# Output projection of a gated cross-attention layer: partial sums kept in DRAM by accumulating transfers

## The chip, the core and the metric

The kernel runs on one core of one Trainium2 chip. The metric is the device time of one execution in microseconds. TensorE (PE) multiplies, VectorE (DVE), ScalarE (ACT) and GpSimd (POOL) work on tiles, SyncE (SP) issues transfers; they run beside each other and wait for one another by semaphores.

## What is computed

A layer with cross-attention and a low-rank expert layer, in fp32, over 16 batches of 128 tokens of width 1024. The change touches the last product of the first line and its sum with x:

```python
NUM_HEADS, NUM_KV_HEADS, HEAD_DIM, HIDDEN = 32, 8, 128, 1024
...
q = (hidden_states @ q_proj_w.T).reshape(B, Q, NUM_HEADS, HEAD_DIM).transpose(0, 2, 1, 3)
...
scores = jnp.einsum('bhqd,bhkd->bhqk', q, k) * scale + attention_mask
attn = jax.nn.softmax(scores.astype(jnp.float32), axis=-1).astype(q.dtype)
out = jnp.einsum('bhqk,bhkd->bhqd', attn, v)
out = out.transpose(0, 2, 1, 3).reshape(B, Q, NUM_HEADS * HEAD_DIM)
return out @ o_proj_w.T
...
x = x + jnp.tanh(g_xattn[0]) * _L0_xattn_ref(_layernorm(x, axis=-1), ctx_4096, ...)
x = x + jnp.tanh(g_ffn[0]) * _L0_ffn_ref(_layernorm(x, axis=-1), L0_ffn_A, L0_ffn_B, L0_ffn_Wr)
```

The gate tanh(g_xattn) is already in the heads when they are written, so the projection's results are added to x as they are.

## The kernel before

All large products are cut into 96 **entries** of one shape: activations of a pair of batches (two row blocks of 128) against a 1024 x 1024 block of weights. Each is done as seven products k = 0 to 6 of half size instead of eight, with sums of the operands taken before (`staged` combinations, by `sums` on GpSimd) and of the results after (`ev`, `usum`). Every operand is split into a high and a low part (`s_hi`, `s_lo` of the activations, `t_hi`, `t_lo` of the weights), and a product is 4 x 3 matmuls of 128 x 512 (lines 715 to 717). The results go to four PSUM banks, `BANK_OF = (0, 1, 2, 3, 0, 2, 3)`.

The entries stand in a fixed order: 16 for keys and values, 32 for queries (with the attention interleaved), 32 for the output projection (O0 to A0, q = 0 to 31), 8 and 8 for the experts. The output projection runs over four **slices** of the 4096 head columns, each over the 8 pairs: slice q // 8, with weights `t` that stay for 8 entries. The result of a pair is the sum over its four slices and x.

Each engine runs its own written-out order, entry by entry and within an entry by position j = 0 to 6, the number of the product that PE is at:

- PE does product k when `s_lo` and (in the first entry of a set) `t_lo` of k are there and the bank is free.
- SP refills the weights `t_raw[k]` (1 MB) in the last entry of a set, each when its product is done, since `t_raw` lies on `t_lo`; at j = 1 it issues the staging of the next entry (1 MB in two transfers, `staged`), all on one queue, and around it the stores and loads of sums.
- ACT casts `s_hi` and `t_hi`, and takes product 0 into `ev`.
- VectorE subtracts for `s_lo` and `t_lo`, and takes the products 1 to 6 out of the banks.
- GpSimd makes the sums of the staged activations, and adds `usum` twice and `ev` once to the sums of the pair.

The seven weights of a new set are due at positions 4, 5, 6 of the set's last entry and 0, 2, 3, 4 of the next (`FILL_POSITIONS`).

The running sums of a pair (1 MB) are in one of two SBUF buffers `acc`, loaded before the entry (`sums_in`, in two halves, from x in slice 0) and stored after it (`sums_out`). The order of the pairs turns round at each slice (`pair_of`), so that the last two pairs of a slice are the first two of the next and stay in SBUF: at q % 8 = 6 and 7 nothing is stored, at 0 and 1 nothing is loaded. q = 0 and 1 write their results without adding; their x is added in DRAM later by `x_into_sums`, two accumulating transfers per pair from GpSimd's queue. After the last slice the rows are normalised and transposed (`finish`).

## Time and profile before

| | us |
|---|---|
| median of 3 executions | 2381.99 (2379.24 to 2382.4) |
| profiled execution | 2379.71 |
| its span, first to last instruction | 2377.9 |
| output projection, q = 2 to 31 | 1391 to 2012 of the span |
| PE busy | 2278.4 (96%) |
| VectorE, ScalarE, GpSimd busy | 1611.9, 1172.6, 1317.3 |

The profile is of one execution. Busy time of an engine is the time in which one of its instructions runs; the matmuls of PE are pipelined and overlap, so their distance from start to start counts, not their length. Where an engine sat idle before an instruction, the view names what ended the wait. "issue" is a wait for which the profile shows no releaser.

### The profile page before, as it was taken

The page shows a single profiled execution, that of the slowest core. Times are in us where ns is not written, and L with a number is a line of the kernel's source. Part 1 is how long each engine was busy: PE and PEld are TensorE (multiplying, and loading weights), DVE is VectorE, ACT ScalarE, POOL GpSimd, SP SyncE. Part 2 cuts the span into 40 slices and gives each one's busy share as a digit, 9 for nine tenths or more (in the row PEclk, how much of TensorE's full clock was granted, in tenths as well). Part 3 has the DMA queues.
Part 4 walks back from the last instruction along what each step waited for, and adds up shares of the span by engine and source line. Part 5 has one row for each costly group of instructions (what it writes and reads, how often), then busy time and mean ns, then how long its engine had stood idle before and what let it go on. Part 6 is the DMA issues. An engine that isn't in the chain of part 4 may idle for free.

```text
span 2377.9 us, 35655 instructions
## 1 busy us (share of the span) xinstructions
PE 2278.4 (96%) x11600; PEld 1911.7 (80%) x11600; DVE 1611.9 (68%) x2649; ACT 1172.6 (49%) x3751; POOL 1317.3 (55%) x1823
## 2 busy tenths in 40 slices
PE   5998999999999989999999899899899999999899
PEld 4886887888888878888888788688687787788687
DVE  6557557777777797777777845755756877544755
ACT  4546546666666676666666722422423334332421
POOL 5566668655565566555555645554655765434321
PEclk8999999999999999999999999999999999999999
DMA  4687556757757457642222545555456466324643
GB/s 170 217 228 268 187 159 231 216 163 198 197 165 198 131 193 195 194 126 89 89 93 95 191 165 177 203 180 202 151 168 238 142 210 253 121 72 144 228 169 133
DMA packets 180231, 412.98 MB, mean 174 GB/s; under 512 B 12176, under 2 KB 77968, under 8 KB 164624
## 3 DMA queue, kind: packets, MB, share of 16 engines
q1 hardware_dynamic: 175440, 379.24, 46.6%
q0 software_dynamic: 4608, 31.46, 7.4%
q8 instruction: 95, 1.56, 0.3%
q14 instruction: 88, 0.72, 0.1%
HBM read 293.21 MB, written 178.26 MB: 198 GB/s over the span
## 4 chain that ended last, share of the span: by engine, by line
PE 86%; POOL 4%; issue 3%; DVE 3%; DMA 3%; ACT 1%; SPq 0%; POOLq 0%; ACTq 0%; DVEq 0%
PE bank L715 24%; PE bank L717 23%; PE bank L716 23%; PE bank L773 4%; PE bank L781 2%; PE bank L761 2%; PE bank L798 1%; PE bank L797 1%; PE bank L796 1%; DVE t_lo L1239 1%; DMA staged<-heads 1%; POOL staged L1696 1%; POOL s_hi L1706 1%; DMA staged<-in_w_q 1%; PE bank L813 1%
## 5 line engine op out<-in xcount | busy, mean ns | idle before, releaser
L715 PE MATMUL bank<-t_hi,s_hi 128*128 128x512 f32 x2688 | 1091.3, 406 | 81.1 <-issue 42.7
L717 PE MATMUL bank<-t_hi,s_lo 128*128 128x512 f32 x2688 | 1059.3, 394 | 0.0
L716 PE MATMUL bank<-t_lo,s_hi 128*128 128x512 f32 x2688 | 1056.1, 393 | 0.0
L715 PEld LDWEIGHTS bank<-t_hi,s_hi 128*128 128x128 f32 x2688 | 510.3, 190 | 189.0 <-issue 85.4
L1239 DVE TENSOR_TENSOR s_lo<-staged,s_hi 128x512 fp32r<-128x512 f32 x672 | 538.2, 846 | 99.6 <-ACT s_hi L962 92.0
L717 PEld LDWEIGHTS bank<-t_hi,s_lo 128*128 128x128 f32 x2688 | 508.8, 189 | 112.0
L716 PEld LDWEIGHTS bank<-t_lo,s_hi 128*128 128x128 f32 x2688 | 510.9, 190 | 91.0
L962 ACT CAST s_hi<-staged 128x512 fp32r<-128x512 f32 x434 | 250.2, 623 | 342.7 <-DMA staged<-heads 181.0
L1679 POOL TENSOR_SCALAR small<-small 128x4 f32<-128x4 f32 (+1 forms) x192 | 66.3, 345 | 414.5 <-ACT small L1051 338.4
L1694 POOL TENSOR_TENSOR staged<-staged 128x512 f32<-128x512 f32 x96 | 139.3, 1451 | 271.1 <-DMA staged<-heads 97.6
L1239 DVE TENSOR_TENSOR t_lo<-t_raw,t_hi 128x2048 fp32r<-128x2048 f32 x70 | 183.2, 2625 | 34.2 <-ACT t_hi L951 25.1
L1364 DVE SCALAR_TENSOR_TENSOR probs<-bank,small,mask 128x128 f32<-128x128 f32 x512 | 144.1, 343 | 89.6 <-POOL small L1686 43.8
L1057 ACT ACTIVATE probs<-probs,small 128x128 f32<-128x128 f32 x512 | 197.5, 386 | 14.1 <-DVE small L1368 14.1
L1045 ACT ACTIVATE bank<-bank 128x128 f32<-128x128 f32 x512 | 135.6, 265 | 113.8 <-PE bank L761 113.8
L1768 POOL TENSOR_TENSOR sums<-sums,usum 128x512 f32<-128x512 f32 x60 | 91.4, 1544 | 175.6 <-DVE usum L1253 175.6
L1038 ACT ACTIVATE heads<-bank,small 128x512 f32<-128x512 f32 x128 | 88.2, 689 | 185.1 <-PE bank L798 183.9
L971 ACT COPY ev<-bank 128x512 f32<-128x512 f32 x96 | 56.1, 585 | 203.5 <-PE bank L717 191.6
L1706 POOL CAST s_hi<-staged 128x512 fp32r<-128x512 f32 x238 | 153.8, 716 | 1.3 <-PE bank L717 1.3
L1696 POOL TENSOR_TENSOR staged<-staged 128x512 f32<-128x512 f32 x96 | 146.9, 1531 | 7.5
L1697 POOL TENSOR_TENSOR staged<-staged 128x512 f32<-128x512 f32 x96 | 150.1, 1563 | 0.0
L773 PEld LDWEIGHTS bank<-keys,queries 128*128 128x128 f32 x1024 | 133.5, 191 | 14.0 <-issue 4.8
L1700 POOL TENSOR_TENSOR staged<-staged 128x512 f32<-128x512 f32 x96 | 137.9, 1436 | 0.0
(131 smaller groups left out, 2961.7 us busy)
## 6 DMA issues: line engine op xcount, KB each, us to landing
heads<-heads SPq DMA_DIRECT2D x128, 256.0 KB, 3.7
t_raw<-combos SPq DMA_DIRECT2D x28, 1024.0 KB, 10.2
t_raw<-in_sets SPq DMA_DIRECT2D x25, 1024.0 KB, 9.6
staged<-in_w_q SPq DMA_DIRECT2D x32, 768.0 KB, 5.9
staged<-heads SPq DMA_DIRECT2D x32, 768.0 KB, 5.9
sums<-sums SPq DMA_DIRECT2D x18, 1024.0 KB, 7.9
sums<-sums SPq DMA_DIRECT2D x36, 512.0 KB, 4.6
xt<-x_columns SPq DMA_DIRECT2D x8, 1792.0 KB, 7.2
```

What stands on the lines that cost most here:

```text
L715: nc.tensor.matmul(out, s_hi[w][:, cols], high, start=start, stop=False, skip_group_check=True)
L716: nc.tensor.matmul(out, s_hi[w][:, cols], low, start=False, stop=False, skip_group_check=True)
L717: done = nc.tensor.matmul(out, s_lo[w][:, cols], high, start=False, stop=at == 3, skip_group_check=True)
L773: done = nc.tensor.matmul(bank[6][:, b * S:b * S + S], qt[j][:, b, :], kg[blk][:, b, :], start=True, stop=True)
L962: nc.scalar.copy(s_hi[k][:, :], staged[:, k, :]).then_inc(s_hi_done, 1)
L1057: done = nc.scalar.activation(pr[i % 3][:, b, :], pr[i % 3][:, b, :], ACT.Exp, bias=nmax[w][:, b:b + 1], accum_out=rsum[w][:, b:b + 1])
L1239: return nc.vector.tensor_tensor(out, whole, hi.bitcast(FP32), ALU.subtract)
L1364: done = nc.vector.scalar_tensor_tensor(pr[i % 3][:, b, :], bank[6][:, b * S:b * S + S], q_rstd[w][:, b:b + 1], mask[:, :], ALU.mult, ALU.add)
L1694: nc.gpsimd.tensor_tensor(staged[:, 2, :], staged[:, 3, :], staged[:, 6, :], ALU.subtract).then_inc(s_sum, 1)
L1696: nc.gpsimd.tensor_tensor(staged[:, 1, :], staged[:, 2, :], staged[:, 0, :], ALU.subtract).then_inc(s_sum, 1)
L1697: nc.gpsimd.tensor_tensor(staged[:, 3, :], staged[:, 0, :], staged[:, 3, :], ALU.subtract).then_inc(s_sum, 1)
L1706: nc.gpsimd.tensor_copy(s_hi[k][:, :], staged[:, k, :]).then_inc(s_hi_done, 1)
```

## The change

In the slices 0 to 2 (`in_dram(q)`, q < 24) an entry no longer adds to sums in SBUF. It writes its own results into `acc[q % 2]` as q = 0 and 1 did (products 3, 5, 6 by VectorE, product 4 now by a copy on ACT), and GpSimd's queue adds the tile to the pair's sums in DRAM by one accumulating transfer of 1 MB. The sums in DRAM are first set to x, by 16 transfers of 0.5 MB that SP issues during the query entries n = 18 to 25. GpSimd's three additions per entry, the stores, the loads of the slices 0 to 2 and `x_into_sums` are gone. In the last slice the sums are loaded for all eight pairs, in one transfer each, and the additions stay. All slices take the pairs in the same order. Semaphores, buffer parities and the tiles laid over `acc` later follow from this.

```diff
     def pair_of(q):
-        return 7 - q % 8 if (q // 8) % 2 else q % 8
-    def sums_loaded(q):
-        return q % 8 >= 2
+        return 7 - q % 8
+    def in_dram(q):
+        return q < 24
     def parts_added(q):
-        return 3 * max(q - 1, 0)
-    def sums_stored(q):
-        return q < 24 and q % 8 < 6
-    def sums_before(q):
-        return q - (1 if q % 8 == 0 else 3)
+        return 3 * (q - 23)
+    def added_before(q):
+        return min(q, 24 + q % 2) // 2
     def loads_up_to(q):
-        return len([p for p in range(q + 1) if sums_loaded(p) and pair_of(p) % 2 == pair_of(q) % 2])
-    def stores_before(q):
-        return len([p for p in range(q) if sums_stored(p) and pair_of(p) % 2 == pair_of(q) % 2])
+        return (q - 24) // 2 + 1
...
-        def sums_out(q):
-            e, b = O0 + q, pair_of(q) % 2
-            for c, k in ((0, 4), (2, 5), (3, 6)):
-                sp.wait_ge(taken[c], plan.after[e, k])
-            if parts_added(q):
-                sp.wait_ge(o_sum, parts_added(q))
-            sp.dma_start(d.sums[pair_of(q)], acc[b][:, :, :]).then_inc(acc_out[b], 16)
+        def sums_start(i):
+            for w in range(2):
+                out = d.sums[i, :, 2 * w:2 * w + 2, :].rearrange("p c q -> p (c q)")
+                sp.dma_start(out, d.x[tiles(i)[w]]).then_inc(sums_set, 16)
         def sums_in(q):
-            b = pair_of(q) % 2
+            b = q % 2
             if q < 26:
-                sp.wait_ge(acc_out[b], 16 * stores_before(q))
+                sp.wait_ge(acc_out[b], 16 * added_before(q))
             else:
                 sp.wait_ge(f_norm, 2 * (q - 25))
-                sp.wait_ge(f_out[q % 2], 32 * ((q - 26) // 2 + 1))
-            if q in (14, 15):
-                sp.wait_ge(x_added[pair_of(q)], 32)
-            for w in range(2):
-                half = acc[b][:, 2 * w:2 * w + 2, :]
-                if q < 8:
-                    sp.dma_start(half.rearrange("p c q -> p (c q)"), d.x[tiles(pair_of(q))[w]]).then_inc(acc_in[b], 16)
-                else:
-                    sp.dma_start(half, d.sums[pair_of(q), :, 2 * w:2 * w + 2, :]).then_inc(acc_in[b], 16)
+                sp.wait_ge(f_out[b], 32 * ((q - 26) // 2 + 1))
+            sp.dma_start(acc[b][:, :, :], d.sums[pair_of(q)]).then_inc(acc_in[b], 16)
...
                     combo_copy(e, r == 3)
-                if n == 33 and r == 2:
-                    sums_out(0)
-                if n == 33 and r == 3:
-                    sums_in(2)
+                if 18 <= n < 26 and r == 0:
+                    sums_start(n - 18)
         heads_out(127)
...
                     stage(e + 1, e)
-                    if sums_stored(q - 1):
-                        sums_out(q - 1)
-                if j == (3 if q < 25 else 5) and q < 31 and sums_loaded(q + 1):
+                if j == (3 if q < 24 else 5) and 23 <= q < 31:
                     sums_in(q + 1)
...
                 act.wait_ge(taken[3], plan.after[e - 1, 3])
-                if O0 + 2 <= e - 1 < A0:
+                if O0 + 24 <= e - 1 < A0:
                     act.wait_ge(o_sum, parts_added(e - 1 - O0))
...
             act.wait_ge(prod, plan.prod[O0 + q, 4])
-            act.wait_ge(s_done, 128 if q else 126)
-            nc.scalar.copy(acc[q][:, 0, :], bank[0][:, :]).then_inc(taken[0], 1)
+            if q < 2:
+                act.wait_ge(s_done, 128 if q else 126)
+            else:
+                act.wait_ge(acc_out[q % 2], 16 * added_before(q))
+            nc.scalar.copy(acc[q % 2][:, 0, :], bank[0][:, :]).then_inc(taken[0], 1)
...
                     first_product(e)
+                if j == 4 and in_dram(q):
+                    sums_tile(q)
                 fill_s(e, after_start(e, j))
...
         def sums_tile(q, k):
-            if k != 5 or q == 0:
+            if q >= 2:
+                dve.wait_ge(acc_out[q % 2], 16 * added_before(q))
+            elif k != 5 or q == 0:
                 if k == 6 and q:
                     dve.wait_ge(pt_done, 127)
                 else:
                     dve.wait_ge(s_done, {3: 128 if q else 125, 5: 126, 6: 127}[k])
             at = {3: 3, 5: 1, 6: 2}[k]
-            {3: result22, 5: result12, 6: result21}[k](O0 + q, acc[q][:, at, :])
+            {3: result22, 5: result12, 6: result21}[k](O0 + q, acc[q % 2][:, at, :])
...
-            b, e = pair_of(q) % 2, O0 + q
+            b, e = q % 2, O0 + q
             at = {3: 3, 4: 0, 5: 1, 6: 2}[k]
             dve.wait_ge(prod, plan.prod[e, k])
-            if k == 3 and sums_loaded(q):
-                dve.wait_ge(acc_in[b], 32 * loads_up_to(q))
-            elif k == 3:
-                dve.wait_ge(o_sum, parts_added(sums_before(q)))
-            if k == 4 and not sums_loaded(q):
-                dve.wait_ge(taken[0], plan.after[O0 + sums_before(q), 4])
+            if k == 3:
+                dve.wait_ge(acc_in[b], 16 * loads_up_to(q))
             if k > 4:
                 dve.wait_ge(o_sum, parts_added(q - 1) + k - 4)
             (minus if k == 3 else plus)(acc[b][:, at, :], acc[b][:, at, :], k)
         def rows2(f, w):
-            b, e, n = (7 - f) % 2, O0 + 24 + f, 2 * f + w
+            b, e, n = f % 2, O0 + 24 + f, 2 * f + w
             if w:
...
             for j in SEVEN:
-                if j == 0 and q == 2:
-                    sums_tile(1, 6)
-                if j == 0 and q > 2:
-                    add_sums(q - 1, 6)
+                if j == 0:
+                    (sums_tile if in_dram(q - 1) else add_sums)(q - 1, 6)
                 if j == 1:
                     second_product(e)
                 if j == 2:
                     third_product(e)
-                if j in (3, 4, 5):
+                if j in (3, 5) and in_dram(q):
+                    sums_tile(q, j)
+                if j in (3, 4, 5) and not in_dram(q):
                     add_sums(q, j)
...
-            b, e = pair_of(q) % 2, O0 + q
+            b, e = q % 2, O0 + q
             if j == 1:
-                if sums_loaded(q):
-                    pool.wait_ge(acc_in[b], 32 * loads_up_to(q))
-                else:
-                    pool.wait_ge(taken[2], plan.after[O0 + sums_before(q), 5])
-                    pool.wait_ge(taken[3], plan.after[O0 + sums_before(q), 6])
+                pool.wait_ge(acc_in[b], 16 * loads_up_to(q))
                 pool.wait_ge(taken[1], plan.after[e, 1])
...
-        def x_into_sums(i):
-            pool.wait_ge(acc_out[i], 16)
-            for w in range(2):
-                nc.gpsimd.dma_start(d.sums[i, :, 2 * w:2 * w + 2, :].rearrange("p c q -> p (c q)"), d.x[tiles(i)[w]],
-                                    accum_op=ALU.add, max_dma_last_dim=4096).then_inc(x_added[i], 16)
+        def sums_out(q):
+            b, e = q % 2, O0 + q
+            for c, k in ((0, 4), (2, 5), (3, 6)):
+                pool.wait_ge(taken[c], plan.after[e, k])
+            if q == 0:
+                pool.wait_ge(sums_set, 256)
+            if q >= 2:
+                pool.wait_ge(acc_out[b], 16 * added_before(q))
+            nc.gpsimd.dma_start(d.sums[pair_of(q)], acc[b][:, :, :], accum_op=ALU.add, max_dma_last_dim=8192).then_inc(acc_out[b], 16)
...
                 finish(plan.beat0[e] + j)
-                if j == 1:
+                if j == 1 and in_dram(e - O0 - 1):
+                    sums_out(e - O0 - 1)
+                if j == 1 and not in_dram(e - O0):
                     add_sums(e - O0, j)
-                if j == 5 and e - O0 in (5, 6):
-                    x_into_sums(e - O0 - 5)
                 if j == 3:
                     sums(e + 1)
-                    add_sums(e - O0, j)
+                    if not in_dram(e - O0):
+                        add_sums(e - O0, j)
                     if e == O0 + 10:
```

Where the instructions stand now is seen at the change from slice 1 to slice 2 (q = 15 to 16). ACT, before: from its cast of weights 3 on, through the first entry of the new slice.

```order
L951 CAST t3_hi_58<-t3_raw_60 128x2048 [waits t_in3]
L962 CAST s_hi_70<-staged_72 128x512 [waits staged_in,product]
L951 CAST t4_hi_61<-t4_raw_63 128x2048 [waits t_in4]
L951 CAST t5_hi_64<-t5_raw_66 128x2048 [waits t_in5]
L951 CAST t6_hi_67<-t6_raw_69 128x2048 [waits t_in6]
L962 CAST s_hi_70<-staged_72 128x512 [waits staged_in,product]
```

ACT, in the changed kernel, the same place.

```order
L931 CAST t3_hi_58<-t3_raw_60 128x2048 [waits t_in3]
L942 CAST s_hi_70<-staged_72 128x512 [waits staged_in,product]
L931 CAST t4_hi_61<-t4_raw_63 128x2048 [waits t_in4]
L931 CAST t5_hi_64<-t5_raw_66 128x2048 [waits t_in5]
L1009 COPY sums0_112<-bank0 128x512 [waits sums_out0,product]
L931 CAST t6_hi_67<-t6_raw_69 128x2048 [waits t_in6]
```

The copy of product 4 (bank 0) of q = 16 now stands between the casts of weights 5 and 6; likewise the copy of q = 15 stands before the cast of weights 0. VectorE, before: from the low part of weights 4 to the result of product 5 of q = 16.

```order
L1239 TENSOR_TENSOR t4_lo_62<-t4_raw_63,t4_hi_61 128x2048 [waits t_hi_done]
L1257 TENSOR_TENSOR sums0_112<-sums0_112,bank3 128x512 [waits o_sum,product]
L1239 TENSOR_TENSOR t5_lo_65<-t5_raw_66,t5_hi_64 128x2048 [waits t_hi_done]
L1253 TENSOR_TENSOR sums0_112<-sums0_112,bank0 128x512 [waits taken_a,product]
L1239 TENSOR_TENSOR t6_lo_68<-t6_raw_69,t6_hi_67 128x2048 [waits t_hi_done]
L1253 TENSOR_TENSOR sums0_112<-sums0_112,bank2 128x512 [waits o_sum,product]
```

VectorE, in the changed kernel.

```order
L1224 TENSOR_TENSOR t4_lo_62<-t4_raw_63,t4_hi_61 128x2048 [waits t_hi_done]
L1242 TENSOR_TENSOR sums0_112<-ev_73,bank3 128x512 [waits taken_c,product,sums_out0]
L1224 TENSOR_TENSOR t5_lo_65<-t5_raw_66,t5_hi_64 128x2048 [waits t_hi_done]
L1224 TENSOR_TENSOR t6_lo_68<-t6_raw_69,t6_hi_67 128x2048 [waits t_hi_done]
L1246 TENSOR_TENSOR sums0_112<-bank2,usum_74 128x512 [waits product,sums_out0]
```

The result of product 4 is gone from between the low parts of weights 5 and 6. GpSimd, before: one entry, from the sums of the staged activations on.

```order
L1694 TENSOR_TENSOR staged_72<-staged_72 128x512 [waits staged_in]
L1696 TENSOR_TENSOR staged_72<-staged_72 128x512 [waits s_sum]
L1697 TENSOR_TENSOR staged_72<-staged_72 128x512
L1700 TENSOR_TENSOR staged_72<-staged_72 128x512 [waits s_sum,staged12_in]
L1771 TENSOR_TENSOR sums0_112<-sums0_112,ev_73 128x512 [waits taken_d]
L1768 TENSOR_TENSOR sums1_113<-sums1_113,usum_74 128x512 [waits taken_b,taken_d,taken_c]
```

GpSimd, in the changed kernel.

```order
L1677 TENSOR_TENSOR staged_72<-staged_72 128x512 [waits staged_in]
L1679 TENSOR_TENSOR staged_72<-staged_72 128x512 [waits s_sum]
L1680 TENSOR_TENSOR staged_72<-staged_72 128x512
L1683 TENSOR_TENSOR staged_72<-staged_72 128x512 [waits s_sum,staged12_in]
L1761 DMA sums<-sums0_112 128x2048 [waits taken_d,sums_out0,taken_c,taken_a]
```

The additions are gone; the issue of the accumulating transfer waits for the last result tile of the entry before and stands ahead of the sums of the next.

## Rows read from the trace of the kernel before

**Rows 1.** The page: busy us (share of span) and instructions of each engine.

```profile
PE 2278.4 (96%) x11600; PEld 1911.7 (80%) x11600; DVE 1611.9 (68%) x2649; ACT 1172.6 (49%) x3751; POOL 1317.3 (55%) x1823
```

**Rows 2.** Windows: stretch, length, busy of PE, PEld, DVE, ACT, POOL, clock, DMA.

```profile
1391.00:1551.00 160.00, 153.31 (x658) 124.85 (x657) 95.29 (x107) 45.59 (x66) 85.64 (x59) 0.98 0.57 186
1551.00:1716.00 165.00, 157.53 (x689) 128.51 (x688) 105.12 (x115) 51.60 (x75) 91.92 (x60) 1.00 0.52 179
...
870.00:1150.00 280.00, 278.97 (x1635) 241.94 (x1634) 212.32 (x431) 183.66 (x780) 165.23 (x310) 1.00 0.51 141
```

**Rows 3.** Timeline of SP's queue: start, length, refills behind products 0 and 1.

```profile
1488.83 0.33 SPq L437 DMA_DIRECT2D t_raw<-in_sets  x1
...
1652.37 0.33 SPq L437 DMA_DIRECT2D t_raw<-in_sets  x1
...
1655.09 0.32 SPq L437 DMA_DIRECT2D t_raw<-combos  x1
...
1813.82 0.33 SPq L437 DMA_DIRECT2D t_raw<-in_sets  x1
```

**Rows 4.** Timeline of PE: first matmuls of products; in brackets idle before.

```profile
1512.72 0.77 PE L715 MATMUL bank<-t_hi,s_hi 128*128 128x512 f32 x1 [3.26 <-issue]
...
1532.32 0.47 PE L715 MATMUL bank<-t_hi,s_hi 128*128 128x512 f32 x1 [0.29 <-issue]
...
1674.19 0.47 PE L715 MATMUL bank<-t_hi,s_hi 128*128 128x512 f32 x1 [2.81 <-issue]
...
1687.21 0.47 PE L715 MATMUL bank<-t_hi,s_hi 128*128 128x512 f32 x1 [1.51 <-issue]
...
1693.80 0.47 PE L715 MATMUL bank<-t_hi,s_hi 128*128 128x512 f32 x1 [0.30 <-issue]
...
1835.17 0.47 PE L715 MATMUL bank<-t_hi,s_hi 128*128 128x512 f32 x1 [2.03 <-issue]
...
1854.77 0.47 PE L715 MATMUL bank<-t_hi,s_hi 128*128 128x512 f32 x1 [0.30 <-issue]
```

**Rows 5.** Timeline of ACT: casts that waited for the staging, casts of weights.

```profile
1504.58 0.62 ACT L962 CAST s_hi<-staged 128x512 fp32r<-128x512 f32 x1 [6.32 <-DMA staged<-heads]
...
1665.08 0.62 ACT L962 CAST s_hi<-staged 128x512 fp32r<-128x512 f32 x1 [6.03 <-DMA staged<-heads]
...
1679.19 5.52 ACT L951 CAST t_hi<-t_raw 128x2048 fp32r<-128x2048 f32 x3
...
1824.93 0.62 ACT L962 CAST s_hi<-staged 128x512 fp32r<-128x512 f32 x1 [4.25 <-DMA staged<-heads]
```

**Rows 6.** Timeline of VectorE at T2.

```profile
1674.02 2.38 DVE L1239 TENSOR_TENSOR s_lo<-staged,s_hi 128x512 fp32r<-128x512 f32 x2
1676.32 2.28 DVE L1239 TENSOR_TENSOR t_lo<-t_raw,t_hi 128x2048 fp32r<-128x2048 f32 x1
...
1679.12 1.28 DVE L1239 TENSOR_TENSOR s_lo<-staged,s_hi 128x512 fp32r<-128x512 f32 x2
...
1684.32 2.78 DVE L1239 TENSOR_TENSOR t_lo<-t_raw,t_hi 128x2048 fp32r<-128x2048 f32 x1
...
1690.32 0.67 DVE L1253 TENSOR_TENSOR sums<-sums,bank 128x512 f32<-128x512 f32 x1
```

**Rows 7.** Timeline of GpSimd at T2: its additions to the sums.

```profile
1671.91 3.33 POOL L1771 TENSOR_TENSOR sums<-sums,ev 128x512 f32<-128x512 f32 x1
1683.37 4.88 POOL L1768 TENSOR_TENSOR sums<-sums,usum 128x512 f32<-128x512 f32 x2 [8.13 <-DVE usum L1253]
```

**Rows 8.** The page, DMA queues: packets, MB, share of 16 engines; q0 is GpSimd's.

```profile
q1 hardware_dynamic: 175440, 379.24, 46.6%
q0 software_dynamic: 4608, 31.46, 7.4%
```

**Rows 9.** GpSimd's issues from x at T1; the landings of all transfers on combos.

```profile
1488.37 1.64 POOL L1777 DMA_DIRECT2D sums<-in_x  x2
```

```profile
DMA to landing us min/median/max: 4.8/9.0/15.0
```

More of the change, by code:

```diff
@@ L296, in program @@
     end = max(end, m.at)
-    ring = [m.over(f"ranks{w}", [P, HALF], acc_at + (w + 4) % 8 * HALF * 4) for w in range(8)]
+    ring = [m.over(f"ranks{w}", [P, HALF], acc_at + w * HALF * 4) for w in range(8)]
     gc = m.over("gated_columns", [P, 4, HALF], xr2_at)
     yr = [[m.over("y_rows00", [P, HIDDEN], xo2_at), m.over("y_rows01", [P, HIDDEN], xo2_at + HIDDEN * 4)],
-          [m.over("y_rows10", [P, HIDDEN], acc_at + 2 * HIDDEN * 4), m.over("y_rows11", [P, HIDDEN], acc_at + 3 * HIDDEN * 4)]]
+          [m.over("y_rows10", [P, HIDDEN], acc_at), m.over("y_rows11", [P, HIDDEN], acc_at + HIDDEN * 4)]]
     ct = [m.over(name, [P, HALF], rw_at + w * HALF * 4) for w, name in enumerate(("c22", "c12", "c21"))]
@@ L328, in program @@
     acc_in, acc_out = [sem(f"sums_in{w}") for w in range(2)], [sem(f"sums_out{w}") for w in range(2)]
-    x_added = [sem(f"x_added{w}") for w in range(2)]
+    sums_set = sem("sums_set")
     o_sum, f_out = sem("o_sum"), [sem(f"f_out{w}") for w in range(2)]
@@ L556, in finish @@
                     for w in range(2):
-                        sp.dma_start(d.x2[tiles(p)[w]], acc[p % 2][:, 2 * w:2 * w + 2, :].rearrange("p c q -> p (c q)")).then_inc(f_out[f % 2], 16)
+                        sp.dma_start(d.x2[tiles(p)[w]], acc[f % 2][:, 2 * w:2 * w + 2, :].rearrange("p c q -> p (c q)")).then_inc(f_out[f % 2], 16)
                 if at == 9:
@@ L1413, in normalise2 @@
         def normalise2(f, w):
-            b = (7 - f) % 2
+            b = f % 2
             dve.wait_ge(f_step, 5 * (2 * f + w + 1))
@@ L1830, in _ @@
                     queries(i)
+                if n == 33 and r == 1:
+                    sums_out(0)
                 if r == 2:
```

## Prediction, made before the changed kernel was run

> **What bounds the kernel now.** I read the page first: TensorE (PE) is busy 96% of the span, the other engines 49 to 68% [rows 1]. A change that takes work from VectorE (DVE) and GpSimd (POOL) can therefore only win where PE waits for them. So the next view was the table of windows over the first two slices of the output projection [rows 2]: PE is idle 6.7 and 7.5 us (160 less 153.31, 165 less 157.53; matmuls overlap, so more is lost than this). Then PE's own instructions there, looking for gaps in their starts. A product of 12 matmuls takes 2.72 us (the refills behind products 0 and 1, 1652.37 and 1655.09, [rows 3]), an entry of seven 19.0, and the only gaps of PE are around q = 7, 15 and 23, where the next entry's products need new weights. I call these T1, T2 and T3.
>
> At each, everything is counted from R, the issue of the first refill of weights, which comes when product 0 of the slice's last entry is done: 1488.83, 1652.37 and 1813.82 [rows 3]. Twelve products of 2.72 later, at R + 32.7 with no idle, PE should start the last product (6) of the new slice's first entry. It starts it at 1532.32, 1693.80 and 1854.77 [rows 4], that is at R + 43.5, 41.4 and 41.0: 10.8, 8.7 and 8.3 us are lost, 28 us in all, and that is all that the three slices can give back.
>
> The loss has two parts. The first is **the landing L of the next entry's activations** (staged), seen where ScalarE (ACT) stops waiting for that DMA: 1504.58, 1665.08, 1824.93 [rows 5], or R + 15.75, 12.7 and 11.1. From L the sums on GpSimd, ACT's cast of k = 1, its cast of weights 1 and VectorE's low part follow one another, and product 1 starts at 1512.72, 1674.19 and 1835.17 [rows 4]: L + 8.1, 9.1 and 10.2. The second is **VectorE's chain from product 1 to product 6**: it is 19.6 us in all three (1532.32 - 1512.72, 1693.80 - 1674.19, 1854.77 - 1835.17), against 13.6 us of PE's five products. VectorE has no gap in it [rows 6].
>
> **What the change takes from the chain.** In the slices 0 to 2 GpSimd's three additions per entry go, and VectorE's result of product 4 becomes a copy on ACT. In ordinary entries this is worth nothing: PE has no idle there. In the chain of T2 I read [rows 6, 7]: the pair of low parts at 1674.02 takes 2.38 us beside GpSimd's addition of 1671.91 to 1675.24; such a pair takes 1.28 us when GpSimd is quiet (1679.12), so 1.1 us goes. The weights' low part at 1684.32 takes 2.78 beside the additions of 1683.37, and the next of its kind takes the same (two alike, one row stands); at 1676.32 with GpSimd quiet it is 2.28: twice 0.5. The result of product 4 at 1690.32 delays what is behind it by 0.6. Together 2.7 us, which would make 16.9 of 19.6.
>
> But the order on ACT gives most of it back. Before, its casts of weights 4, 5 and 6 stand in one row and are done early. Now the copy of product 4 of the new entry stands before the cast of weights 6, so that cast waits until PE has done product 4. From PE's start of product 4: product 2.7, copy 0.6, cast 1.9 [rows 5], low part 2.3, product 6 starts at + 7.5, where now it is 6.6 (1693.80 less 1687.21) [rows 4]. Product 4 itself comes at 13.0 after product 1 now (1687.21 - 1674.19) and at 13.0 - 1.1 - 0.5 = 11.4 then. **The chain is 11.4 + 7.5 = 18.9 at T1 and T2**, a gain of 0.7 and not 2.7. At T3 the new slice is the last, which keeps its additions and VectorE's result of product 4, so neither the copy nor the other gains are there, only the 1.1: 18.5. From L to product 1 I take 8.3: the new landing (below) is later, when VectorE's first low part of weights is done, as at T1 (8.1) and not as at T2 and T3 (9.1, 10.2). That low part itself moves, since ACT now casts weights 0 behind its copy of product 4 (R + 10.9): cast done at R + 13.4, low part at R + 15.7. Product 0 needs it and starts later, but product 1 waits longer anyway, so this costs nothing as long as L is above about R + 15; below it would cost up to 1 us.
>
> The slower of two passes on the shared memory port fits a rule: the Trainium skill, SBUF — State Buffer, section SBUF: two separate sides, says that VectorE with two SBUF inputs and a GpSimd instruction that reads SBUF exclude one another for the whole instruction. By this rule the gain is that of the missing GpSimd instructions alone, and the 2.28 against 2.78 us agrees in sign, though not with a full block.
>
> **What the change adds.** The store and the load of sums (2 MB an entry, plain) become one accumulating transfer of 1 MB. Its price: the accumulating queue moved 30 transfers of 1 MB (28 of combos, 2 from x) with 7.4% of 16 engines' span [rows 8], 0.074 x 2377.9 / 30 = 5.9 us each; the plain queue needed 0.466 x 2377.9 / 379.24 = 2.9 us per MB, 3.1 for the 1.05 MB of one transfer. So an accumulation holds the engines about as long as the store and the load did together, and in an ordinary entry (19 us, one staging of 3 us) all of it hides. Nothing waits for it soon: buffer q % 2 is written again 30 us later.
>
> But before, the order of the pairs left entries 7, 8, 15, 16, 23 and 24 without a store, and 8, 9, 16, 17, 24 and 25 without a load. Now **an accumulation starts in every one of the transition entries**, about 2 us ahead of the first refill: POOL issues it when VectorE has written the last tile of entry q - 1, R - 2.3, and needs 0.8 us for one [rows 9]. About 1.4 us of it run before the refills; the other 4.5 share the engines with refills 0 and 1 and delay the staging behind them on SP's queue. Added to T3's 11.1, the one with nothing in the way, this gives L = R + 15.6. T1 already shows the case: the two transfers from x are issued at 1488.37, half a us before R [rows 9], and L is R + 15.75; they go, and so does the load of sums in front of them, so with the earlier start of 0.9 us it gives 14.9. T2 would be 12.7 + 4.5 = 17.2 at most. I take 15.3 for all three. If the transfer from SBUF cost only the plain 3.1, 1.7 would be left: 12.8 from T3. So L lies between R + 12.8 and 17.2.
>
> For T3, the load of the sums of q = 24 comes too, behind refill 3; refill 6 lands later by 3 us, and VectorE reaches it at R + 39, so it is covered. The load of q = 25 (after the accumulation of q = 23, R + 35, landing at R + 42) is wanted at R + 50. The start of the sums, 16 transfers of 0.5 MB from x into DRAM, goes to 870 to 1150 us, where PE is busy 279.0 of 280 us and waits for no DMA [rows 2]; from 0 to 3 us, I take 0.5. GpSimd's new waits (for VectorE's last tile) stand in front of its sums for the next entry, whose data come 10 us later; nothing of those is held up.
>
> **The sum.** Start of product 6 after the change, from R: T1 and T2 15.3 + 8.3 + 18.9 = 42.5, T3 15.3 + 8.3 + 18.5 = 42.1. Against 43.5, 41.4 and 41.0: -1.0, +1.1, +1.1, together +1.2; with +0.5, **+1.7 us**. The profiled execution took 2379.71 (span 2377.9), the median of three is 2381.99; I add to the median: 2383.7. A measurement of this kernel can tell about 0.2%, 4.8 us, from no change.
>
> **Rivals.** (1) *Slower: the staging lands later than I think.* Each us of L counts three times. The sum is zero at L = R + 14.7 and slower by over 4.8 us from L = R + 16.3. At R + 17.2, T2's upper bound for all three, it is +7.4: 2389.4. For it: accumulations took up to 15.0 us from issue to landing [rows 9]. Against: T1 had the same megabyte starting later and landed at 15.75. A lowered clock may come with the longer idle of PE (the stretch of T1 has a mean granted clock of 0.98, the one of T2 1.00 [rows 2]), but the chain behind T1 was 19.6 us all the same, so it is hidden again.
> (2) *Faster: an accumulation out of SBUF costs no more than a plain transfer.* L = R + 12.8, the sum 1.7 - 7.5 = -5.8: 2376.2. Against it stand the 5.9 us; for it only that those all came from DRAM. The Trainium skill, DMA: Bandwidth & Descriptors, section Anatomy of one DMA, fits 2.0 us plus bytes at 436 GB/s for a transfer issued by GpSimd and has no surcharge for accumulating; by it a megabyte holds the engines 2.4 us, which is this rival, and the queue's row speaks against it.
> (3) *The chain does not shrink at all*, because an ACT cast or a refill sets its pace: 0.7 + 0.7 + 1.1 more, +4.2: 2386.2. Against: VectorE has no gap in it up to product 4, so what is taken from it there must come out.
>
> **Chances.** Forecast (L within 14 and 16.2, sum -2.2 to +4.4): 0.50. Rival 1 with L above 16.3: 0.24. Rival 2 and what lies toward it: 0.16, of which 0.13 pass -4.8. Rival 3: 0.10, half of it over +4.8 by the spread of L. From these: faster by over 0.2% 0.13, within 0.2% 0.58, slower 0.29. The range goes from 2375.5 to 2390, the lower end at rival 2, the upper at rival 1; the forecast's own is 2380 to 2386.5.
>
> **What would show it.** Right: a start of product 6 near R + 42 at all three, earlier than now at T1 and later at T2 and T3; L near R + 15; the pair of low parts at 1.3 us and a wait of VectorE for ACT before the last low part of weights; accumulations of 5 to 6 us of engine time each. Wrong: any gap of PE in an ordinary entry, a GpSimd or ACT wait for a sums transfer, PE losing time between 870 and 1150 us, or L outside 12.8 to 17.2.

## The result: slower by about 6 us

The changed kernel takes 2387.09 us, median of 13 executions (2383.62 to 2393.8), and the kernel before 2381.25 (13 executions, 2378.55 to 2384.92). The ratio is 1.003, 95% interval 1.0021 to 1.0038: slower by 5.0 to 9.0 us. The same kernel again, 8 executions on another occasion, gave 2389.0 against 2380.97, a ratio of 1.0035 (1.0024 to 1.0045). The forecast was 2383.7, likeliest within 0.2%. Both medians lie outside the forecast's own 2380 to 2386.5, and both are over 0.2% slower than before; they are inside the whole range of 2375.5 to 2390, whose upper end was set by a rival that did not occur.

### The profile page after: what moved, and what is told of

It is laid out like the page before. It is cut to its first block, busy times and chain, and to the rows that moved or that the text cites. A ratio compares the mean times of both kernels' runs of the same rounds, so it can differ in the third digit from the quotient of the medians.

```text
span 2392.0 us, 35572 instructions
## 1 busy us (share of the span) xinstructions
PE 2291.0 (96%) x11600; PEld 1922.1 (80%) x11600; DVE 1582.6 (66%) x2627; ACT 1182.1 (49%) x3773; POOL 1218.7 (51%) x1777
## 3 DMA queue, kind: packets, MB, share of 16 engines
q0 software_dynamic: 7488, 54.53, 12.6%
## 4 chain that ended last, share of the span: by engine, by line
PE 86%; DVE 3%; issue 3%; POOL 3%; DMA 3%; ACT 2%; SPq 0%; POOLq 0%; ACTq 0%; DVEq 0%
PE bank L695 24%; PE bank L697 24%; PE bank L696 24%; PE bank L753 4%; PE bank L761 2%; PE bank L741 2%; DVE t_lo L1224 1%; PE bank L778 1%; PE bank L777 1%; PE bank L776 1%; DVE s_lo L1224 1%; DMA staged<-heads 1%; DMA staged<-in_w_q 1%; ACT t_hi L931 1%; POOL staged L1679 1%
## 5 line engine op out<-in xcount | busy, mean ns | idle before, releaser
L1224 DVE TENSOR_TENSOR s_lo<-staged,s_hi 128x512 fp32r<-128x512 f32 x672 | 523.5, 824 | 115.6 <-ACT s_hi L942 107.1
L1677 POOL TENSOR_TENSOR staged<-staged 128x512 f32<-128x512 f32 x96 | 130.5, 1360 | 421.6 <-DMA staged<-heads 245.6
L1680 POOL TENSOR_TENSOR staged<-staged 128x512 f32<-128x512 f32 x96 | 149.6, 1558 | 0.0
L1679 POOL TENSOR_TENSOR staged<-staged 128x512 f32<-128x512 f32 x96 | 145.2, 1512 | 7.5
L1683 POOL TENSOR_TENSOR staged<-staged 128x512 f32<-128x512 f32 x96 | 142.7, 1486 | 0.0
L753 PE MATMUL bank<-keys,queries 128*128 128x128 f32 x1024 | 135.3, 275 | 1.6 <-DVE probs L1351 1.6
## 6 DMA issues: line engine op xcount, KB each, us to landing
t_raw<-combos SPq DMA_DIRECT2D x28, 1024.0 KB, 11.8
```

The costliest lines, as they stand in the source:

```text
L753: done = nc.tensor.matmul(bank[6][:, b * S:b * S + S], qt[j][:, b, :], kg[blk][:, b, :], start=True, stop=True)
L1224: return nc.vector.tensor_tensor(out, whole, hi.bitcast(FP32), ALU.subtract)
L1679: nc.gpsimd.tensor_tensor(staged[:, 1, :], staged[:, 2, :], staged[:, 0, :], ALU.subtract).then_inc(s_sum, 1)
L1680: nc.gpsimd.tensor_tensor(staged[:, 3, :], staged[:, 0, :], staged[:, 3, :], ALU.subtract).then_inc(s_sum, 1)
L1683: nc.gpsimd.tensor_tensor(staged[:, 5, :], staged[:, 4, :], staged[:, 1, :], ALU.add).then_inc(s_sum, 1)
```

## The profile after

The page of the changed kernel, engines and queues (as [rows 1, 8]), and its issues of accumulations (count, KB each, median us to landing):

```profile
PE 2291.0 (96%) x11600; PEld 1922.1 (80%) x11600; DVE 1582.6 (66%) x2627; ACT 1182.1 (49%) x3773; POOL 1218.7 (51%) x1777
...
q1 hardware_dynamic: 169392, 351.97, 42.9%
q0 software_dynamic: 7488, 54.53, 12.6%
...
sums<-sums POOLq DMA_DIRECT2D x24, 1024.0 KB, 8.0
```

The work went as meant: VectorE is busy 29 us less, GpSimd 99 us less, 27 MB fewer pass the plain queue. GpSimd's queue holds 52 transfers of 1 MB where it held 30: the 24 new ones, the 28 of combos, and no longer the two from x. They hold the engines 0.126 x 2392.0 / 52 = 5.8 us each on average; with the 28 at 5.9 as before, the 24 out of SBUF come to 5.7 each, as forecast. None of this is where the time is made; PE's busy time went up by 12.6 us with the same 11600 matmuls, so matmuls ran longer. The windows over the first two slices, columns as in [rows 2], show that and the clock:

```profile
1391.00:1551.00 160.00, 152.28 (x645) 124.14 (x645) 86.27 (x101) 48.89 (x72) 51.66 (x41) 0.96 0.55 150
1551.00:1716.00 165.00, 157.10 (x664) 127.97 (x663) 88.87 (x103) 53.48 (x80) 53.35 (x41) 0.96 0.53 147
```

The granted clock is 0.96 in both, where before it was 0.98 and 1.00. SP's queue dates the transitions T1, T2 and T3, and the next refill of weights after them, in the last entry of the last slice, called T4 here (as [rows 3]):

```profile
1490.88 0.34 SPq L431 DMA_DIRECT2D t_raw<-in_sets  x1
...
1657.69 0.33 SPq L431 DMA_DIRECT2D t_raw<-in_sets  x1
...
1825.02 0.33 SPq L431 DMA_DIRECT2D t_raw<-in_sets  x1
...
1997.10 0.33 SPq L431 DMA_DIRECT2D t_raw<-in_sets  x1
```

From R of T1 to that of T4 it is 506.2 us; before it was 495.9 (163.5 + 161.5 + 170.9). This is 10.3 of the 14.1 us between the two profiled executions (spans 2392.0 and 2377.9). Of the rest 2.1 us lie before T1 and 1.7 behind T4. This execution was the slowest of its 13. The second profiled execution of the same kernel has a span of 2386.6, 8.7 more than before: 4.1 from T1 to T4 (500.0 us), 4.2 before T1 and 0.4 behind T4. What lies before T1 is mostly scatter: the last matmul of the attention stage starts 1389.2 to 1393.4 us after the start in the eleven profiles of all kernels here, and the profile before is the earliest. Its mean is 1390.8 in the three profiles of the kernel before and its variants and 1392.0 in the eight of the changed kernel and its variants, so up to about 1.2 us may belong to the change; that is not shown. The differences of the medians, +5.8 and +8.0, lie between the +4.1 and the +10.3 of the two profiles from T1 to T4.

PE's products 1, 4 and 6 at T1 (compare [rows 4]), with the second and third matmul of product 6:

```profile
1514.51 0.77 PE L695 MATMUL bank<-t_hi,s_hi 128*128 128x512 f32 x1 [3.26 <-issue]
...
1526.02 0.47 PE L695 MATMUL bank<-t_hi,s_hi 128*128 128x512 f32 x1 [0.31 <-issue]
...
1534.91 0.76 PE L695 MATMUL bank<-t_hi,s_hi 128*128 128x512 f32 x1 [3.09 <-issue]
1535.47 0.63 PE L696 MATMUL bank<-t_lo,s_hi 128*128 128x512 f32 x1
1535.90 0.63 PE L697 MATMUL bank<-t_hi,s_lo 128*128 128x512 f32 x1
```

Product 6 comes after an idle of 3.09 us, which was 0.29 before, and from its second matmul on they start 0.43 us apart: 512 columns at 1.2 GHz. The chain to it, on ACT in the timeline:

```profile
1529.06 0.59 ACT L1009 COPY sums<-bank 128x512 f32<-128x512 f32 x1 [6.94 <-PE bank L697]
1529.54 1.91 ACT L931 CAST t_hi<-t_raw 128x2048 fp32r<-128x2048 f32 x1
```

On VectorE:

```profile
1531.48 3.33 DVE L1224 TENSOR_TENSOR t_lo<-t_raw,t_hi 128x2048 fp32r<-128x2048 f32 x1 [2.76 <-ACT t_hi L931]
```

And on GpSimd, which sums the next entry's activations:

```profile
1531.39 1.27 POOL L1679 TENSOR_TENSOR staged<-staged 128x512 f32<-128x512 f32 x1
1532.63 3.33 POOL L1680 TENSOR_TENSOR staged<-staged 128x512 f32<-128x512 f32 x1
```

ACT stood 6.94 us for product 4 with the cast of weights 6 behind it, as the forecast said; VectorE then waited 2.76 us for that cast. Its low part took 3.33 us and not 2.3. GpSimd was in an addition until 1532.66, and 1532.66 + 2.2 is when the low part is done; GpSimd's next addition, which takes 1.3 us when VectorE does not hold it up, took 3.33, that is until 1.2 us after the low part. In the second execution this addition of GpSimd starts at R + 39.4 and not R + 40.5, and ends 0.2 us after the low part has begun. GpSimd's timeline there:

```profile
1532.47 1.29 POOL L1679 TENSOR_TENSOR staged<-staged 128x512 f32<-128x512 f32 x1
```

VectorE's timeline in the second execution:

```profile
1533.57 2.35 DVE L1224 TENSOR_TENSOR t_lo<-t_raw,t_hi 128x2048 fp32r<-128x2048 f32 x1 [2.77 <-ACT t_hi L931]
```

And PE's, the first matmul of product 6:

```profile
1536.02 0.47 PE L695 MATMUL bank<-t_hi,s_hi 128*128 128x512 f32 x1 [2.12 <-issue]
```

Product 6 came at R + 42.97 there (R was 1493.05) after an idle of 2.12, at full clock. The rule of the Trainium skill that the prediction quoted (SBUF — State Buffer, section SBUF: two separate sides: VectorE with two SBUF inputs and a GpSimd instruction that reads SBUF exclude one another for a whole instruction) is borne out by these rows. The prediction read [rows 6] as less than a full block, and that was wrong: at T2 before, the low part began at 1684.32, the GpSimd addition that was running (1683.37, 1.59 us) ended at 1684.96, and 0.6 us of rest and 2.2 of its own make the 2.78. The same timeline of VectorE has a third such low part, that of weights 6:

```profile
1690.92 2.78 DVE L1239 TENSOR_TENSOR t_lo<-t_raw,t_hi 128x2048 fp32r<-128x2048 f32 x1
```

It began while GpSimd's first sum of the next entry's activations was running (1688.21, 3.34 us), 0.6 us before its end, and those sums stay in the changed kernel.

The windows of 10 us from product 6 on, at T1 and T2, show what the clock did. The kernel before:

```profile
1532.00:1542.00 10.00, 9.71 (x44) 8.03 (x44) 9.71 (x11) 3.92 (x7) 6.69 (x5) 1.00 0.00 0
1694.00:1704.00 10.00, 10.00 (x45) 8.26 (x45) 9.40 (x10) 3.91 (x7) 6.69 (x5) 1.00 0.01 2
```

The changed kernel:

```profile
1534.00:1544.00 10.00, 9.09 (x28) 7.32 (x29) 6.08 (x7) 1.19 (x3) 4.51 (x3) 0.66 0.13 13
1701.00:1711.00 10.00, 8.97 (x27) 7.13 (x28) 5.11 (x7) 0.34 (x1) 2.94 (x2) 0.66 0.13 15
```

Its second execution:

```profile
1536.00:1546.00 10.00, 9.98 (x44) 8.30 (x45) 7.69 (x10) 2.77 (x5) 3.63 (x3) 1.00 0.33 53
...
1699.00:1709.00 10.00, 9.72 (x36) 7.94 (x37) 6.73 (x9) 2.77 (x5) 3.88 (x3) 0.83 0.27 41
```

All together, us from R:

| | forecast | profile after T1; T2; T3 | second profile |
|---|---|---|---|
| staging landed | 15.3 | 15.1; 15.6; 15.1 | 15.3; 15.7; 15.5 |
| product 1 | 23.6 | 23.6; 23.8; 23.6 | 23.6; 23.9; 23.7 |
| product 6 | 42.5; 42.5; 42.1 | 44.0; 44.3; 42.1 | 43.0; 43.3; 42.2 |
| product 6 to next R, less before's | 0 | +2.7; +3.0; 0.0 | 0.0; +1.5; 0.0 |

Product 6 of the changed kernel comes +0.5, +2.9 and +1.2 us later than before, the lower clock behind it adds 2.7 and 3.0: 10.3, the whole difference. In the second execution -0.52, +1.82, +1.23 and +1.55 give 4.1. Two experiments below keep ACT's order and fit: there the stretch behind product 6 is 0.0 us longer at a granted clock of 1.00, 1.5 and 1.8 at 0.83, and 2.8 at 0.70.

## Experiments

**The same kernel again**, for a second profile:

> The changed kernel as it is, for a second profile: the first one came from its slowest execution (2393.8 where the median is 2387.1). If the 3 us at the lower clock behind T1 and T2 belong to the change, they are there again (stretches of 166 to 167.5 us from R to the next R, against 163.5 and 161.5 before), and the rest of the span is that of before, so about 2387. If they were an accident of that execution, the stretches are 164 and the total is nearer to 2384.

2389.0 us (2386.03 to 2392.78, 8 executions); its profile is read above. The time is that of the first case, but the stretches of the profiled execution are not: 163.0 from T1 to T2, with no lower clock, and 164.8 from T2 to T3. So the loss at the lower clock comes and goes from one execution to the next.

**1. The copy behind the cast.** The changed kernel, with ACT's copy of product 4 moved behind the cast of weights 6.

```diff
-                if j == 4 and in_dram(q):
-                    sums_tile(q)
                 fill_s(e, after_start(e, j))
...
                 fill_t(plan.beat0[e] + j)
+                if j == 4 and in_dram(q):
+                    sums_tile(q)
```

> The changed kernel with one edit: in an entry of the slices 0 to 2 ACT's copy of product 4 stands behind its cast of weights of the same position, not before it. Theory A (the cast of weights 6 that waits for product 4 is what costs): at T1 and T2 the time from product 1 to product 6 goes from 20.4 us to about 17, the idle of 3.1 us before product 6 goes, and with it the 3 us that PE loses behind it at the lower clock. Two times (3.4 + 2.9) = 12.6 us off: about 5 to 7 us faster than before, near 2375. Rival B (the time goes to the accumulations beside the refills, the order of ACT is hidden): L stays at R + 15 and the time at 2385 to 2388.

2379.54 us (2376.97 to 2381.92, 11), ratio to before 0.9996 (0.9987 to 1.0005), and 7.5 us less than the changed kernel. That is the kernel before again and not the 5 to 7 us faster that were expected. The staging lands where it did (R + 15.3, 16.1, 15.3). ACT's timeline at T1:

```profile
1528.89 0.59 ACT L1009 COPY sums<-bank 128x512 f32<-128x512 f32 x1 [5.01 <-PE bank L697]
```

VectorE's:

```profile
1526.29 4.48 DVE L1224 TENSOR_TENSOR t_lo<-t_raw,t_hi 128x2048 fp32r<-128x2048 f32 x2
```

The copy waits as before, but the last two low parts stand in one row (2.2 us each) without a wait, PE has no idle before product 6, and the stretches T1 to T2 and T2 to T3 take 160.5 and 161.3 us where after took 166.8 and 167.3. Less 120.0 from product 6 to the next R, product 6 of T1 is at R + 40.4, 16.9 after product 1 (R + 23.5), and that of T2 17.1 after it: the 16.9 that the prediction had for the chain without ACT's order. Most of what was gained at the chains is lost by the late landing, which stays as in the changed kernel: product 6 is 3.1 us earlier than before at T1, 0.1 at T2 and 1.1 later at T3, so from T1 to T4 it is 493.8 us against 495.9. So the order of two ACT instructions made the slowdown.

**2. The wait alone, in the kernel before.** ACT waits for product 4 before it casts weights 6, at q = 8 and 16:

```diff
                 fill_s(e + 1, before_next(e, j))
+                if j == 4 and q in (8, 16):
+                    act.wait_ge(prod, plan.prod[e, 4])
                 fill_t(plan.beat0[e] + j)
```

> The kernel before with one wait added: in the first entries of slices 1 and 2 (q = 8, 16) ACT waits for product 4 before it casts weights 6. No transfer and no addition changes. Theory A: product 6 starts 7.5 to 9 us after product 4 and not 6.6, with an idle of about 3 us before it, and PE loses 3 us at the lower clock behind it: +4 to +5 us at each, 2389 to 2391 where before is 2381. Rival B (the wait is hidden): no difference, 2381.

2383.12 us (2381.38 to 2387.78, 11), ratio 1.0008 (1.0 to 1.0017): +2 us (0 to 4), far less than the 8 to 10 expected. Product 6 at T1 in PE's timeline:

```profile
1536.40 0.47 PE L715 MATMUL bank<-t_hi,s_hi 128*128 128x512 f32 x1 [1.67 <-issue]
```

The two windows of 10 us behind product 6, at T1 and T2:

```profile
1536.00:1546.00 10.00, 9.60 (x42) 7.99 (x43) 9.01 (x11) 2.77 (x5) 5.11 (x4) 1.00 0.00 0
1699.00:1709.00 10.00, 9.81 (x43) 8.18 (x44) 8.96 (x11) 2.77 (x5) 5.13 (x4) 1.00 0.01 2
```

The wait moved product 6 by 1.0 and 1.4 us (R + 44.5 and 42.8), 2.4 us in all, which agrees with the measured 2, and the clock stayed at 1.00 after an idle of 1.67 us. Here the rest of the chain is slow too, so product 4 is late and the wait for it opens a short hole. In the changed kernel the low parts ahead are done sooner, the hole is 2.1 to 3.1 us, and what was saved comes out as idle. The expectation had wrongly given this wait the price of the clock as well.

**3. The start of the sums.** The kernel before with the 16 copies of x into (unused) DRAM that the change adds, issued by SP for the eight entries from 18 on:

```diff
+                if 18 <= n < 26 and r == 0:
+                    spare_start(n - 18)
```

> The kernel before with the 16 transfers of 0.5 MB from x into DRAM added in the query entries n = 18 to 25, into a buffer that nobody reads. Prediction's price: 0 to 3 us, 0.5 taken. Theory A (hidden): within 0.5 us of before, PE's busy time from 870 to 1150 us stays at 279. Rival B (the profiled 2 us that the changed kernel is late at 1371 us come from these): +2 us, and the last matmul of the attention starts at 1371.7, not 1369.8.

2380.68 us (2378.29 to 2386.13, 11), ratio 1.0005 (0.9996 to 1.0014). They cost nothing that can be told (the interval goes from -1 to +3.3 us). From 870 to 1150 us PE waits 2.5 us in all where before it waited 1.0, each time for VectorE and not for a transfer.

**4. A plain store instead of an accumulation.** The changed kernel without the adding, so the sums lack x and the other slices:

```diff
-            nc.gpsimd.dma_start(d.sums[pair_of(q)], acc[b][:, :, :], accum_op=ALU.add, max_dma_last_dim=8192).then_inc(acc_out[b], 16)
+            nc.gpsimd.dma_start(d.sums[pair_of(q)], acc[b][:, :, :]).then_inc(acc_out[b], 16)
```

> The changed kernel with plain stores in place of the accumulating ones, on the same queue and at the same places: the sums in DRAM hold only the last slice stored, so this leaves out the additions of x and of two slices. Theory A (an accumulation holds the DMA engines twice as long as a plain transfer of its size): L goes from R + 15.1 to about 12.5 to 13.5, product 1 comes 2 us earlier at T1 to T3, and the time falls by about 6 us to 2381. The wait of the cast of weights 6 for product 4 stays, and so the idle of 3 us before product 6 at T1 and T2. Rival B (it is the order on the queues, not the price of adding): L stays at 15 and the time at 2387.

2385.99 us (2382.9 to 2387.97, 7), ratio 1.0024 (1.0013 to 1.0035): the interval overlaps the changed kernel's, though a gain of 6 us was expected. GpSimd's queue on the page:

```profile
q0 software_dynamic: 7488, 54.53, 9.6%
```

GpSimd's first sum at T1, where R is 1492.48:

```profile
1504.33 1.30 POOL L1677 TENSOR_TENSOR staged<-staged 128x512 f32<-128x512 f32 x1 [12.32 <-DMA staged<-heads]
```

ACT's cast of weights 0:

```profile
1503.85 1.91 ACT L931 CAST t_hi<-t_raw 128x2048 fp32r<-128x2048 f32 x1
```

VectorE's low part of them:

```profile
1505.80 3.35 DVE L1224 TENSOR_TENSOR t_lo<-t_raw,t_hi 128x2048 fp32r<-128x2048 f32 x1 [4.40 <-ACT t_hi L931]
```

And product 6 on PE:

```profile
1534.96 0.52 PE L695 MATMUL bank<-t_hi,s_hi 128*128 128x512 f32 x1 [2.94 <-issue]
```

A plain megabyte costs 3.0 us less ((0.126 x 2392.0 - 0.096 x 2386.2) / 24), 2.7 for 5.7, and the staging lands 3.2 us sooner, at R + 11.9 (13.0 at T2). The price was right, its worth was not: with the landing there, ACT is casting weights 0, and VectorE's low part of them meets GpSimd's sums (3.35 us against 2.3). Product 6 comes at R + 42.5 and 43.3, 1.5 and 1.0 us before the profile after, and 0.5 before and level with its second one, and the idle before it, 2.94 us, is still ACT's order. So the accumulation's longer transfer is not what made the change slow.

**5. Accumulations behind the transition.** At q = 7, 15 and 23 GpSimd issues the accumulation behind its sums of the next entry's activations, and SP loads the sums of q = 24 at j = 6 instead of 3; with experiment 1's order on ACT, and without it.

```diff
-                if j == 1 and in_dram(e - O0 - 1):
+                if j == 1 and in_dram(e - O0 - 1) and e - O0 not in (7, 15, 23):
                     sums_out(e - O0 - 1)
...
                     sums(e + 1)
+                    if e - O0 in (7, 15, 23):
+                        sums_out(e - O0 - 1)
...
-                if j == (3 if q < 24 else 5) and 23 <= q < 31:
+                if j == (6 if q < 24 else 5) and 23 <= q < 31:
```

> As the first, and at q = 7, 15 and 23 GpSimd issues the accumulating transfer behind its sums for the next entry, so behind the landing of the staging; the load of the sums of q = 24 goes behind the last refill. Theory A (the accumulation delays the landing L from R + 11 to 13 to R + 15): L is back at R + 11 to 13, product 1 comes 3 us earlier at each of T1 to T3, another 5 to 9 us off: 2366 to 2371. Rival B (the refills are delayed instead, and VectorE or ACT waits for them): L is back, but product 6 stays where the first kernel has it, 2375.

> The changed kernel with the late accumulating transfers of the second kernel (q = 7, 15, 23) but with ACT's copy still before the cast of weights. If both causes add up: L = R + 11.4 as there, the idle of 3 us before product 6 and the slow stretch behind it as in the changed kernel, so 2.3 + 5 us at T1 and T2 together above the second kernel's 2376, near 2383. If the late transfer alone were enough: 2376 to 2378.

With the order 2376.13 us (2371.28 to 2378.31, 10), ratio 0.9977 (0.9967 to 0.9986), where 2366 to 2371 was expected. Without it 2388.36 (2384.36 to 2389.97, 5), ratio 1.0033 (1.0021 to 1.0046), where 2383 was expected. With the order the staging now lands at R + 10.8 to 11.2, and the chain from product 1 to 6 is 16.9 and 17.1 at T1 and T2; without it the staging lands at R + 11.6 to 12.0. T1 to T3 takes 313.2 us with both, 321.8 with the order alone, 325.5 with late accumulations alone, 334.1 and 327.8 in the changed kernel. Late accumulations alone did not show in the median, partly for what they cost at T3, in both kernels. VectorE there, with the order:

```profile
1842.00 0.69 DVE L1242 TENSOR_TENSOR sums<-sums,bank 128x512 f32<-128x512 f32 x1 [6.56 <-DMA sums<-sums]
```

And PE behind it:

```profile
1845.49 0.77 PE L695 MATMUL bank<-t_hi,s_hi 128*128 128x512 f32 x1 [6.95 <-issue]
```

The load of the sums of q = 24, issued at 1833.49, is now the last to land: a new wait of 6.56 us on VectorE, 6.95 of idle on PE, and the stretch T3 to T4 is 176.0 us instead of 172.1.

**6. Late accumulations without that wait.** First: experiment 5 with the order, at q = 7 and 15 alone, T3 as in the changed kernel. Second: experiment 5 with all three, and the accumulation of q = 23 moved behind GpSimd's first additions of q = 24.

```diff
-                if j == 1 and in_dram(e - O0 - 1) and e - O0 not in (7, 15, 23):
+                if j == 1 and in_dram(e - O0 - 1) and e - O0 not in (7, 15, 23, 24):
                     sums_out(e - O0 - 1)
...
+                if j == 1 and e - O0 == 24:
+                    sums_out(23)
```

> As the second kernel (copy behind the cast, late accumulations), but at q = 23 transfer and load stand as in the changed kernel. The second kernel lost 7.3 us at q = 24, where VectorE waited for the load of sums. Expected: the stretches from the refills of T1 to T2 and T2 to T3 stay at 156.6 us, the one behind T3 goes from 176.0 to 172.0, so 4 us less: 2372. Rival: the load lands no earlier, 2376.

> As the second kernel, late accumulations at all three, but the accumulating transfer of q = 23 stands on GpSimd behind its additions for q = 24, so behind the landing of that load. The load then has the engines for itself and lands 4 us earlier (R + 33 in place of R + 37.3); the load of q = 25 comes later by as much. Expected if the latter is covered: the stretch behind T3 170 to 172 us, 2370 to 2372. Rival: the wait moves to q = 25, 176 us and 2376.

2372.13 us (2370.6 to 2374.43, 6), ratio 0.9968 (0.9956 to 0.998), and 2370.15 (2368.57 to 2374.24, 5), ratio 0.996 (0.9947 to 0.9972), both as expected. Both beat both kernels, by 8 to 10 us and by 15 to 17; the two are not told apart. At T3 the second one still has a hole. VectorE's timeline there:

```profile
1841.23 0.69 DVE L1242 TENSOR_TENSOR sums<-sums,bank 128x512 f32<-128x512 f32 x1 [3.18 <-PE bank L697]
```

And GpSimd's:

```profile
1841.22 4.56 POOL L1747 TENSOR_TENSOR sums<-sums,usum 128x512 f32<-128x512 f32 x2 [16.50 <-DMA sums<-sums]
```

VectorE's wait is still for the load of the sums, though the view names PE: the instruction takes product 3, which PE had done by 1837.2, and it starts with the GpSimd addition that waited for the same load. The load lands at R + 33.9 where it was R + 37.3 in experiment 5, so the wait is shorter and not gone. T3 to T4 takes 171.7 us, no better than the 171.9 of the first, so nothing is shown to be gained there.

## Why the prediction was right in its parts and short in its sum

The time lies in the stated range partly by luck. The range reached up to 2390 for a late landing (rival 1), which did not happen; what happened was a longer chain and a slower clock behind it, and no rival had the second. The median of 13 before is 2381.25 and not the 2381.99 of three that the forecast was added to, so the forecast +1.7 stands against +5.8 and +8.0.

- **Price and landing: right, in part by luck.** 5.7 us for 5.9; L at 15.1 to 15.7 for 15.3. One input was wrong: the accumulation is issued at R + 0.5 (1491.42 and 1658.05) and not at R - 2.3, since the last tile that GpSimd waits for is written behind four low parts of activations in VectorE's row. By the prediction's first working, T3's 11.1 and all of the 5.9 behind it, such a start would give R + 17.0; its second one, from T1 with the transfers from x issued at the same place, is the one that held. Rival 1 as stated did not occur. The 15.0 us put up for it were no accumulation's: [rows 9] hold all transfers on combos, SP's too, and those from GpSimd's queue landed after 8.1 to 10.8 us. At T1 to T3 the accumulations of the changed kernel took 11.8 to 12.6.
- **From landing to product 1, and T3: right.** 8.2 to 8.6 for 8.3; product 6 of T3 at R + 42.1 and 42.2 for 42.1. The pair of low parts takes 1.28 us, as said.
- **The start of the sums: right** (experiment 3 shows no cost, within -1 to +3.3 us, for 0.5 forecast).
- **The chain at T1 and T2: the step that was mis-sized.** 18.9 was forecast. It is 20.4 and 20.5 in one execution, 19.3 and 19.4 in the other. The order copy, cast, low part is what happened, but "low part 2.3" left out that GpSimd's sums of the next entry run at that moment: 3.33 us in one, 2.35 in the other. The kernel before had such a row at the same place of T2 (1690.92, 2.78 us). The other 0.4 is in the hand-overs from product 4 to copy and from low part to PE (7.9 us from product 4 to product 6 in the second execution, 7.5 forecast).
- **"So it is hidden again": the step that failed.** It was argued from idle before product 1, where VectorE's chain sets the pace of products 1 to 6 and slow matmuls fit into its waits. The idle that the change makes stands before product 6, behind which PE is the bound and nothing hides a slow matmul. Product 6 to the next R took 2.7 and 3.0 us more, in the other execution 0 and 1.5. The premise holds at product 1: before, the clock in the 10 us behind it was 0.69 at T1 and 1.00 at T2, and the chain 19.6 both times. No rival held this: a wait that the forecast itself priced brings a second cost at its end.
- **Rival 2 would not have been one.** With a plain transfer (experiment 4) the landing moved as priced, 3 us, but the kernel by 1.1 us by the medians, which is not told from nothing: the bound from ACT's cast of weights 0, which the prediction named as "up to 1 us", and the port took the rest. "Each us of L counts three times" fails below R + 15 with the change's order on ACT; with the order mended it nearly holds (from experiment 1 to the first of 6, L at T1 goes from 15.3 to 11.6, 3.7 us, and the stretch from 160.5 to 157.2, 3.3 us).
- **Rival 3** gave about the measured chain (19.6) and time (2386.2) by another cause. VectorE's chain shrank to 16.9 as read from [rows 6, 7] as soon as ACT's order was mended (experiment 1).

What stays open: what share of the attention stage's scatter belongs to the change (about 1.2 us by the means of the eleven profiles, within their scatter), and why the clock fell after 1.8 us of idle in one place and not after 3.26 in another (below).

## What to carry to other kernels

When work is moved to an engine with time to spare, look at what stands behind it in that engine's row: a copy that waits for a product, put ahead of a cast that a later product needs, undid a gain of 2.5 to 2.7 us at each of two transitions and made a loss of it, with the engine half idle (ACT is busy 49%). Price a new idle of PE by its place: where another engine sets the pace behind it a lower clock is free, where PE does it comes on top. Put a transfer that nobody waits for soon behind the loads that somebody does; with the order mended that gave some 7 us (2379.54 to 2372.13).

## What the runs showed of the hardware

The granted clock in some 10 us behind a hole of PE before a late product (4 to 6), over all profiles (idle in us, clock): 1.67, 1.00; 1.68, 1.00; 1.77, 1.00; 2.05, 0.83; 2.12, 1.00; 2.19, 0.83; 2.64, 1.00; 2.90, 0.70; 2.94, 0.83; 3.09, 0.66; 3.09, 0.66; 3.57, 0.83; 5.66, 0.78; 6.95, 0.71. The three shortest of these cost no clock and the seven longest all did, but the holes earlier in the same transitions do not keep to that: 1.83 and 1.84 us gave 0.83, 2.81 gave 1.00 once and 0.83 once, and 3.26 before product 1 gave 1.00 three times (in the second profile of the changed kernel, in experiment 1 and in the first of 6) and 0.69 in the kernel before. So between 1.8 and 3.3 us the length of the hole alone does not tell what the clock does. Of the 6.2 us by which the two profiles of one kernel differ between T1 and T4, 4.2 stand behind product 6, where their clocks differ.

VectorE with two SBUF operands and GpSimd's additions in SBUF took turns by whole instructions: 1.2 us of rest of a GpSimd addition and 2.2 of its own made VectorE's 3.33, and the GpSimd addition behind it took 3.33 instead of 1.3. An accumulating transfer of 1 MB out of SBUF held the DMA engines 5.7 us, a plain one from the same queue 2.7 (an estimate from the queue's share in the profile, 12.6% and 9.6%, with 5.9 for each of its 28 other transfers).
